# Output tiles placed in the last steps and around the last softmax, transfers issued by slot, the flag read in slot 11

## The reference, cut to what matters

```python
x = L0_attn_x                       # 4 x 2048 x 512, float32
xn = layernorm(x)
# linear attention, 16 heads of 32, causal: S_kv += k v^T, z += k, with elu + 1 on q and k
num = einsum('bhd,bhde->bhe', qt, S_kv); den = einsum('bhd,bhd->bh', qt, z) + EPS
attn = (num / den) @ wo
# softmax attention, 16 heads, full 2048 keys
q = (q / norm(q) + query_embedding) * softplus(temperature)
h = softmax(q @ k^T / sqrt(32)) @ v
gates = softmax(h @ Wr.T + br); top 3 of 15; sw = softmax(h @ Ws.T + bs)
out = h * (gain made of the top gates and sw)
x = x + attn + (out @ Wp.T + bp)
```

## Time and profile before

| | |
|---|---|
| runs (3) | 4501.65 us median, 4498.16 to 4506.65 |
| profiled execution | 4503.88 us, span 4502.1 us, mean granted TensorE clock 0.966 |
| busy share of the span | PE 90%, DVE 76%, ACT 62%, POOL 7% |
| instructions | 88027 |

### The profile page before, as it was taken

One profiled execution on the slowest core, in us unless ns is written; L12 is line 12 of the kernel. 1 busy time (PEld: TensorE's weight loads), 2 busy tenths in 40 slices (PEclk: granted clock), 3 DMA queues, 4 the chain that ended last, 5 costly groups with the idle time before them and its releaser, 6 DMA issues.

```text
span 4502.1 us, 88027 instructions
## 1 busy us (share of the span) xinstructions
PE 4034.5 (90%) x36076; PEld 1619.0 (36%) x36076; DVE 3408.2 (76%) x3542; ACT 2807.0 (62%) x3831; POOL 326.6 (7%) x210
## 2 busy tenths in 40 slices
PE   3489999999999999999999999999999999999768
PEld 1243333333333333333333333333333333333113
DVE  3637888887888878787878778777877777778763
ACT  3227767676766666666666667666666666666650
POOL 0100000000000001000000100000000000000001
PEclk7689999999999999999999999999999999999999
DMA  3421211212122212222221222222121211211106
GB/s 122 148 79 40 66 51 53 60 52 59 49 81 65 86 57 85 67 64 86 66 85 56 89 68 77 68 70 82 56 71 60 70 56 59 79 58 51 37 29 188
DMA packets 373143, 319.90 MB, mean 71 GB/s; under 512 B 160192, under 2 KB 320960, under 8 KB 372032
## 3 DMA queue, kind: packets, MB, share of 16 engines
q1 hardware_dynamic: 372672, 313.43, 22.9%
HBM read 237.30 MB, written 76.02 MB: 70 GB/s over the span
## 4 chain that ended last, share of the span: by engine, by line
PE 68%; ACT 15%; DVE 8%; issue 6%; DMA 2%; SPq 0%; POOL 0%; ACTq 0%; DVEq 0%
PE ps L961 15%; PE ps L836 15%; PE ps L947 14%; ACT prob L703 12%; PE ps L926 7%; DVE acc L1430 5%; PE ps L844 4%; PE ps L879 3%; PE ps L900 2%; PE ps L902 2%; PE ps L861 2%; PE ps L873 1%; PE ps L887 1%; ACT sq L601 1%; ACT e L640 1%
## 5 line engine op out<-in xcount | busy, mean ns | idle before, releaser
L703 ACT ACTIVATE prob<-ps 128x1024 f32<-128x1024 f32 x2048 | 1985.1, 1023 | 667.6 <-PE ps L947 609.2
L1430 DVE TENSOR_TENSOR acc<-acc,prob 128x2048 f32<-128x2048 f32 x896 | 2047.6, 2285 | 146.8 <-ACT prob L703 131.2
L961 PE MATMUL ps<-prob,v 128*32 128x512 f32 x8192 | 1104.6, 612 | 1.1 <-ACT prob L703 1.1
L947 PE MATMUL ps<-q_hi,k_hi 32*128 32x512 f16 x4096 | 425.5, 387 | 261.5 <-ACT prob L703 194.5
L947 PE MATMUL ps<-q_hi,k_lo 32*128 32x512 f16 x4096 | 416.5, 378 | 1.7 <-issue 1.7
L947 PE MATMUL ps<-q_lo,k_hi 32*128 32x512 f16 x4096 | 415.8, 378 | 0.0
L836 PE MATMUL ps<-x_hi,w_hi 128*128 128x512 f16 x1024 | 400.0, 391 | 6.7 <-issue 4.4
L836 PE MATMUL ps<-x_lo,w_hi 128*128 128x512 f16 x1024 | 397.0, 388 | 0.0
L836 PE MATMUL ps<-x_hi,w_lo 128*128 128x512 f16 x1024 | 394.7, 385 | 0.0
L947 PEld LDWEIGHTS ps<-q_hi,k_hi 32*128 32x128 f16 x4096 | 109.4, 91 | 701.3 <-ACT prob L703 454.9
L926 PE MATMUL ps<-wop_hi,fin 128*128 128x512 f16 x1024 | 325.9, 384 | 3.7 <-DMA fin<-olo_scratch 3.7
(11 more groups left out here) (250 smaller groups left out, 4604.0 us busy)
## 6 DMA issues: line engine op xcount, KB each, us to landing
x_hi<-xhi_scratch SPq DMA_DIRECT2D x64, 512.0 KB, 4.2
x_lo<-xlo_scratch SPq DMA_DIRECT2D x64, 512.0 KB, 5.2
x_in<-in_x SPq DMA_DIRECT2D x64, 256.0 KB, 5.3
rq<-rq_scratch SPq DMA_DIRECT2D x64, 256.0 KB
rdl<-rdl_scratch SPq DMA_DIRECT2D x64, 256.0 KB
rden<-rden_scratch SPq DMA_DIRECT2D x64, 256.0 KB
fin<-hhi_scratch SPq DMA_DIRECT2D x128, 128.0 KB, 3.5
fin<-hlo_scratch SPq DMA_DIRECT2D x128, 128.0 KB, 4.3
```

Source lines behind the costliest of these rows:

```text
L703: s_.activation(prob[i % 3][:, 2 * p:2 * p + 2, :], ps[:, 2 * p:2 * p + 2, :], ACT.Exp, bias=-SHIFT, scale=1.0 / CQK).then_inc(exped, 1)
L947: last = t_.matmul(bank[h], kk[rows32(h), cols128(kt)], qq[rows32(h), :], start=(kk is kh and qq is qh), stop=(kk is kl and not wide))
L961: last = t_.matmul(bank[OUT][rows32(h), :], v[m // NB % 2][:, kt, rows32(h)], prob[i % 3][:, h, :], start=(kt == 0), stop=(kt == TT - 1))
L1430: v_.tensor_tensor(acc[:], acc[:], prob[i % 3][:], ALU.add).then_inc(summed, 1)
```

## The change

Steps 60 to 63 (`LIGHT` = 60) get 3, 1, 3 and 3 output tiles, at slots 4, 8, 12, or 4 alone in step 61; each product is cut in two halves of six matmuls, o in the tile's slot and the next, h in the two behind. Tiles 44 to 53 lie there. Gates of block 12 are in step 62 and of block 13 in step 63, in slots 3 (matmuls), 4 and 5. Step 64 is taken apart: tiles 54 and 55 stand around the last softmax, 56 to 63 behind it. In steps before 60 the gains are made in slot 13 of the gate step. The flag is read in slot 11 on TensorE (behind the last transposes that wait for it) and slot 12 on ScalarE and VectorE, into a register that the branch at the boundary uses. SP's list is ordered by slot. POOL's order stays, with the biases of all tiles of a step first.

```diff
+LIGHT = LAST - NB
+LATE = {LIGHT: (4, 8, 12), LIGHT + 1: (4,), LIGHT + 2: (4, 8, 12), LIGHT + 3: (4, 8, 12)}
+def out_tiles(s):
+    if LIGHT <= s < LAST:
+        return [(n_out(s) + i, slot) for i, slot in enumerate(LATE[s])]
+    return [(n_out(s), 12)] if n_out(s + 1) > n_out(s) else []
+def gate_slot(s):
+    return 11 if s < LIGHT else 3
...
@@ SyncE
-            for s in range(FIRST, LAST + 1):
+            for s in range(FIRST, LAST):
...
-                if out_tile(s - 1) is not None:
-                    store_y(out_tile(s - 1))
-                if n is not None and n + 1 < NBLK:
-                    load_block(n + 1)
...
-                if out_tile(s) is not None:
-                    load_y(out_tile(s))
...
+                for kt in range(TT):
+                    if kt == 0:
+                        if p is not None:
+                            sp.wait_ge(dl_kept, p + 1)
+                            pack(rdl_c, rdl_d, rdl, dl_out, dl_in, p)
+                        if f is not None:
+                            for j in range(BT):
+                                load_use("g", f * BT + j)
+                        if o is not None:
+                            load_use("o", o)
...
+                    if kt == 2:
+                        if mp is not None:
+                            sp.wait_ge(den_kept, mp + 1)
+                            pack(rden_c, rden_d, rden, den_out, den_in, mp)
+                        if p is not None:
+                            sp.wait_ge(rdl_done, p + 1)
+                            spread(rdl, rdl_d, rdl_c[:], rdl_out, rdl_in, p, o1_ready)
+                    if kt == 3:
+                        if out_tiles(s - 1) and out_tiles(s - 1)[-1][1] == 12:
+                            store_y(n_out(s) - 1)
+                        if o is not None:
+                            load_y(o)
...
+                        if n is not None and n + 1 < NBLK:
+                            load_block(n + 1)
+                        if o is not None and f is None:
+                            load_use("h", o)
...
+                    if s >= LIGHT:
+                        for to, slot in out_tiles(s):
+                            if kt == slot + 5:
+                                store_y(to)
+                            if kt == slot - 3:
+                                load_y(to)
+                                load_use("o", to)
+                            if kt == slot - 1:
+                                load_use("h", to)
+            r = REST[0]
+            load_y(r)
+            load_use("o", r)
+            load_use("h", r)
+            load_use("o", r + 1)
+            load_use("h", r + 1)
+            store_y(r - 1)
+            load_y(r + 1)
+            load_use("g", r + 2)
+            sp.wait_ge(den_kept, NBLK)
+            pack(rden_c, rden_d, rden, den_out, den_in, NBLK - 1)
+            load_use("g", r + 3)
+            load_use("g", r + 4)
+            sp.wait_ge(rden_done, NBLK)
+            spread(rden, rden_d, rden_c[:], rden_out, rden_in, NBLK - 1, hm_done)
+            load_use("g", r + 5)
+            store_h_hi(NBLK - 1)
+            store_h_lo(NBLK - 1)
+            for t in range(r + 2, NT):
+                if t % BT == 0 and t > r + 2:
                     for j in range(BT):
+                        load_use("g", t + j)
+                load_use("o", t)
+                load_use("h", t)
+                store_y(t - 2)
+                load_y(t)
@@ TensorE
+            def branch(dst, use, a, ks=range(KC)):
...
+                            if n % NB == NB - 1:
+                                pe.sem_inc(settled, 1)
+                                pe.reg_load(wide_reg, flag[0:1, 0:1])
+                    if s >= LIGHT:
+                        if kt == gate_slot(s) and gate_block(s) is not None:
+                            pe.wait_ge(den_kept, mp + 1)
+                            gates(gate_block(s), X2)
+                        for to, slot in out_tiles(s):
+                            if kt in (slot, slot + 1):
+                                pe.wait_ge(yo_done, to)
+                                branch(X0, ("o", to), 0, (0, 1) if kt == slot else (2, 3))
+                            if kt in (slot + 2, slot + 3):
...
+                                pe.wait_ge(y_done, to)
+                                branch(X1, ("h", to), 1, (0, 1) if kt == slot + 2 else (2, 3))
...
-                pe.wait_ge(flag_ready, ig + 1)
-                pe.sem_inc(settled, 1)
-                wide = pe.value_load(flag[0:1, 0:1], min_val=0, max_val=1)
                 pe.wait_ge(qlo_done, (ig + 1) * NB)
-                with pe.If(wide):
+                with pe.If(wide_reg):
...
+            weigh(NBLK - 1, TT - 1)
+            for t in REST:
+                if t % BT == 0 and t // BT >= n_gated(LAST):
+                    pe.wait_ge(den_kept, NBLK)
+                    pe.wait_ge(lg_kept, t // BT)
+                    gates(t // BT, X2)
+                pe.wait_ge(yo_done, t)
+                branch(X0, ("o", t), 0)
+                if t == REST[0]:
+                    pe.wait_ge(lg_kept, n_gated(LAST))
+                    total(NBLK - 1)
+                pe.wait_ge(y_done, t)
+                branch(X1, ("h", t), 1)
@@ VectorE
-                        if gate_block(s - 1) is not None:
-                            gate_gains(gate_block(s - 1))
+                    if kt == gate_slot(s) + 2 and gate_block(s) is not None:
+                        gate_gains(gate_block(s))
```

More of the change, by code:

```diff
@@ L109 @@
         USES += [("g", gate_block(s_) * BT + j) for j in range(BT)]
[L110 to L115, removed]
+    for t_, _ in out_tiles(s_):
+        USES += [("o", t_), ("h", t_)]
+for t_ in range(n_out(LAST), NT):
+    if t_ % BT == 0 and t_ // BT >= n_gated(LAST):
+        USES += [("g", t_ + j) for j in range(BT)]
+    USES += [("o", t_), ("h", t_)]
 USE_AT = {use: i for i, use in enumerate(USES)}
+REST = range(n_out(LAST), NT)
 def build(nc, x_d, w6_d, wop_d, wg_d, bqkv_d, bp_d, bg_d, temp_d, qe_d, out_d):
@@ L543, in _ @@
                 n, t = prepared(s), norm_tile(s)
-                if out_tile(s) is not None:
-                    add_bias(out_tile(s))
+                for to, _ in out_tiles(s):
+                    add_bias(to)
                 if t is not None:
@@ L781, in _ @@
                         step(s, False)
-            step(LAST, False)
-            for f in range(N_SPREAD, B * NB):
+            keep_out(NBLK - 1)
+            keep_den(NBLK - 1)
+            split_h(NBLK - 1)
+            for f in range(n_gated(LAST), B * NB):
                 gate_exps(f)
@@ L918, in turn_phk @@
                 last.then_inc(phk_turned, 1)
-            def branch(dst, use, a):
+            def branch(dst, use, a, ks=range(KC)):
                 u = USE_AT[use]
                 pe.wait_ge(fin_loaded[u % NFIN], (u // NFIN + 1) * 32)
-                for k in range(KC):
+                for k in ks:
                     for i, w in ((0, wop_hi), (0, wop_lo), (1, wop_hi)):
@@ L1532, in step @@
                             normalise(t)
-                        if gate_block(s - 1) is not None:
-                            gate_gains(gate_block(s - 1))
+                    if kt == gate_slot(s) + 2 and gate_block(s) is not None:
+                        gate_gains(gate_block(s))
+                    if s >= LIGHT:
+                        for to, slot in out_tiles(s):
+                            if kt == slot + 1:
+                                add_o(to)
+                            if kt == slot + 3:
+                                add_h(to)
+                    if kt == 12 and n is not None and n % NB == NB - 1:
+                        dve.wait_ge(flag_ready, n // NB + 1)
+                        dve.sem_inc(settled, 1)
+                        dve.reg_load(wide_reg, flag[0:1, 0:1])
                     if kt == 4 and n is not None:
@@ L1562, in _ @@
             for ig in range(NIG):
[L1563 to L1566 removed]
+                with dve.If(wide_reg):
                     g = ig % NG
@@ L1588, in _ @@
                     step(s)
-            step(LAST)
-            for f in range(N_SPREAD, B * NB):
-                gate_logits(f)
-                gate_gains(f)
-                for j in range(BT):
-                    add_o(f * BT + j)
-                    add_h(f * BT + j)
+            add_up(NBLK - 1, TT - 1)
+            r = REST[0]
+            add_o(r)
+            add_h(r)
+            invert_den(NBLK - 1)
+            add_o(r + 1)
+            add_h(r + 1)
+            divide_h(NBLK - 1)
+            split_h(NBLK - 1)
+            for t in range(r + 2, NT):
+                if t % BT == 0:
+                    gate_logits(t // BT)
+                    gate_gains(t // BT)
+                add_o(t)
+                add_h(t)
 def kernel(**inputs):
```

188 lines of the change are left out of this document (80 added, 108 removed).

## The result

The changed kernel takes **4466.27 us** (median of 4 runs, 4462.62 to 4471.15), against 4504.02 for the kernel before in the same session (4498.16 to 4506.65): ratio 0.9919, 95% interval 0.9901 to 0.9936. It is faster, by 38 us and not by the 74 forecast, and lies outside the range (4396 to 4454). The profiled execution took 4465.83 us.

The account below looks back on a forecast made before the run. TensorE, with two thirds of the span in the chain, was taken as the bound. 4503.88 - 54.0 - 4.6 - 17 + 2 = 4430.3, less 2.2 for the median, gave 4428 us; range 4396 to 4454.

Parts of the forecast that it names:

- Part 1, the tail: Behind the last exponential: 16 tiles become 10, with loads issued ahead; 76.9 us against 130.9, 54.0 less.
- Part 2, the light steps: Steps 60 to 63 take six tiles more, as half products mostly in TensorE's gap, slots of 3.13 us; 4.6 us less.
- The adds of VectorE (0.75 us) and the gate chain hide beside its 2.29 of each slot: Light steps: this VectorE work costs nothing, since an exponential needs only the sum of three slots before; otherwise 1.5 us a tile.
- Part 3, the boundaries: Boundaries between groups: shorter branch and earlier flag read, less the moved gains, net -1.2 us at ten boundaries; sum 17 us less.
- 2.3 us for the transfers: Boundary branch: moving the block load to slot 3, away from the branch's fetch of its target, saves 2.3 us.
- 0.8 for the read: Boundary: reading the flag in slot 11 or 12 takes about 0.8 us off TensorE's queue ahead of the branch.
- (c): Gate steps: the gains moved to slot 13 on VectorE delay add_h and so the branch's start by 1.9 us per boundary.
- it had under a microsecond in hand: Gate steps: TensorE's last product, waiting for add_h, had less than 1 us of room, so the whole +1.9 was counted.
- I leave the 1.51 of the following step as it is: Step behind a boundary: its extra 1.51 us was taken as unchanged, with idle still near 2.5 us.
- Part 4, SP by slot: Full steps: block load, y load and y store move to slot 3, making rstd and query norms 2 to 4 us later; +2.
- I cost it at 0 in the plain ones, and at 0.2 in the ten gate steps: Full steps: VectorE's waiting room takes up the later powers, nothing in plain steps, 0.2 us in each gate step; +2.
- Rival B: Late y load delays bias, rstd and power, making VectorE late in all 44 steps with an output tile; 4516 us, chance 0.04.

Follow-up runs that it names:

- experiment 2: Changed kernel with only the y and o loads for the slot-8 tile of light steps issued ahead of the spread of rden: 4452.18 us.
- the three: Changed kernel with powers ahead of the bias, slot-8 loads ahead of the rden spread, and full-step gains back in slot 3 of the next step: 4412.49 us.
- experiment 13: On top of the three, VectorE takes the reciprocal of rden ahead of gate logits and y add in light steps: 4411.84 us.
- experiment 1: Changed kernel with GpSimd's two small powers (rstd, rn) ahead of the bias add, all else the same: 4457.8 us.
- experiment 4: The run of the three, all its edits together on the changed kernel: 4412.49 us, ratio to before 0.9794.
- experiments 12: On top of the three, y store, block load and y load back at the step's start and the flag read back at the boundary: 4459.83 us.

## Why the prediction was half right

**Part 1, the tail:** right, 54.0 forecast, 54.0 measured, term by term within 1.2 us.

**Part 2, the light steps:** the sum for the half products was right (3.16 us a slot against 3.13; 198.3 us with the loads mended against 197.5). The step that failed is "The adds of VectorE (0.75 us) and the gate chain hide beside its 2.29 of each slot". They hide from the exponentials, but not from SP: the reciprocal behind them holds the spread, and the spread holds the next tile's loads. Price 14 us by experiment 2, 17 to 18 by the profile, against nothing forecast.

**Part 3, the boundaries:** that the branch fetches its target, and that transfers beside it make this longer, was right. The split was not: 2.3 us for the transfers and 0.8 for the read have no meaning, since at ten boundaries neither lengthens the branch by itself. Nor was the sum: to undo both and the rest of that group costs 48.0 us in steps 1 to 59 (3779.6 against 3731.5), where the terms without (c) made 37. The kernel before less the three is only 39.5, since the three carry the second stall of 8.6 us, which the prediction does not have.
(c) was mis-sized too. The mechanism holds: add_h comes 1.9 us later, and "it had under a microsecond in hand" fits the 1.19 us that TensorE then idles, 0.7 short of 1.9. But with the powers mended the gains cost 2.3 us in each gate step (769.0 against 743.8; 2.0 by experiment 13's profile) and not 1.9, and with step 15 and the steps behind the boundaries 34.9 us in all (28.9) against some 21 forecast. "I leave the 1.51 of the following step as it is" did not hold. Part of it is the clock: low behind the branch of all ten gate steps in experiment 1, and high in three of ten in experiment 4.

**Part 4, SP by slot:** this step failed most plainly. "I cost it at 0 in the plain ones, and at 0.2 in the ten gate steps". Plain steps did stay at 62.74, though VectorE waits for GpSimd in nearly all of them. The gate steps paid 15.3 us (784.3 against 769.0), and 29 where the gains are out of the way (772.9 against 743.8). The powers came 4.5 to 6.7 us later, not 2 to 4, and in eight of ten gate steps that was not won back by slot 13. Rival B had the chain right (y load, bias, rstd, power, VectorE) and its place wrong: not 44 steps, but the ones with gates. A chance of 0.04 for it as a whole hid a likely small form of it.

Why half of the gain went: 18 us in the light steps and 21 in steps 1 to 59. There, going from the kernel before to the changed one by way of experiments 12, 4 and 1, the terms are -48.0 (boundary transfers and read), +8.6 (second stall and the rest of 12 against before), +34.9 (gains) and +10.7 (late powers), together +6.2. The last two are worth 10.3 and 35.3 if they are taken in the other order, so only their sum, 45.6, is a number of its own. With both and the loads mended the kernel is at 4412, below the forecast and inside its range.

## What to carry to other kernels

A queue's program order couples things that share no data: when a load or a small operation is moved, write down for every instruction behind it on that queue who waits for it, and price that in the tightest step, not in the average one. Room that swallows a delay in plain steps says nothing of the full ones. Two delays that end at the same wait are neither added nor counted once: here the removal of either gave 10 us and of both 40 to 46, since what is left of one keeps TensorE waiting. A short wait of TensorE can cost more than itself by the clock: in step 31 of the changed kernel a y add 1.9 us late made slots 12 and 13 take 13.3 us instead of 9.3. And a change can cost something where no edit aims: the second stall came with it and shows only in single steps.

## What the runs showed of the hardware

- A TensorE branch ended 1.2 to 1.7 us behind the landing of a 16 KB packet on the instruction queues. It took 3.3 to 4.4 us at ten boundaries with either the flag read or some 1.5 MB of transfers (block, y out, y in) put back beside it, and 5.3 to 6.1 with both; where 1 MB left 3.3 to 3.8 us ahead of it, 5.1 to 6.1 without a read. Its whole price, with the clock behind it and the code of the unused version, was 4.1 us (65.8 over 16), where VectorE's and ScalarE's branches took 0.06 and 0.05.
- TensorE was at the low clock behind an idle time of 2.58 us (ahead of 2332.51) and behind 1.19 and 2.81 in a row. Behind the branch of the ten gate steps 19 to 55 of the three it idled 1.87 to 2.52. The first scores took 0.37 to 0.40 us each in eight, and 0.55 and 0.52 in two, behind 1.89 and 2.02. The eight matmuls of `weigh` behind them took 1.06 us in three steps, behind 1.87, 1.89 and 2.36, and 1.90 to 1.94 in seven. The idle time alone does not tell which.
- In the run with the early y load a VectorE product of eight elements a row took 1.22 us instead of 0.17 while GpSimd's add of 1.28 us ran beside it:

```profile
3644.00 1.28 POOL L603 TENSOR_TENSOR y<-y,bp 128x512 f32<-128x512 f32 x1 [43.63 <-DMA y<-in_x]
```

```profile
3644.08 1.22 DVE L1559 TENSOR_TENSOR share<-z,zrec 128x8 f32<-128x8 f32 x1
```

The Trainium skill (SBUF — State Buffer, "SBUF: two separate sides") says that of a GpSimd operation that reads SBUF and a VectorE operation with two SBUF inputs the one that starts first keeps the shared port for its whole instruction. The trace agrees, here from VectorE's side: GpSimd started 0.08 us earlier, and VectorE ended 0.02 us behind it.
- Still open: in steps 19, 31 and 47 of the three TensorE stalls a second time just behind the branch, 2.06, 3.00 and 2.36 us in the middle of the first scores, and these steps take 68.9 to 70.7 us where most others take 66.2 to 67.2. The kernel before has no such stall there.
